# A LoRA linear layer over eight batches: seven block products per pair of batches instead of eight, and router and attention moved into the second phase

## The chip, the cores and the metric

The kernel runs on 1 core of one Trainium2 chip. Its time is the device time of one execution in microseconds (us). Everything below speaks of that one core: TensorE (PE) multiplies, its weight loads run beside it (PEld), VectorE (DVE), ScalarE (ACT) and GpSimd (POOL) work on tiles of 128 partitions, SyncE (SP) issues loads. ScalarE issues the stores.

## What is computed

Eight batches of 512 tokens with 2048 features go through a linear layer with bias and a LoRA term (rank 16, one adapter for each batch). The result h then goes through a small network. All arrays are float32.

```python
h   = x @ W.T + bias + (x @ A[id].T) @ B[id].T            # D_IN = D_OUT = 2048, rank 16
q   = h @ Wq.T                                            # 64 wide
top, idx = top_k((q @ Wr.T) @ (keys @ Wr.T).T / sqrt(48) + log_rel, 8)
w   = softmax(q . keys[idx] / 8 + log_rel[idx])
aux = (w . values[idx]) @ Wvd.T @ Wvu.T                   # 512 slots, 128, 2048
u   = clip(0.5 * log1p(var(h)) / mean(log1p(var(h))) + 2.5 * sigmoid(gelu(h @ Wu1.T + bu1) @ Wu2.T + bu2), 0, 5)
gate = sigmoid(0.5 * clip((u - 0.5) / 1.5, 0, 1) - 1), 0 where below 0.05
out = x + h + gate * aux
```

The mean of log1p(var) runs over all tokens of all batches. So no gate, and no output, is known before all of h is.

## The kernel before

Every float32 operand of a large product is split into two parts, a rounded one (hi, written by ScalarE, `to_hi`, L426) and the rest (lo, written by VectorE, `lo`, L688). Each product is made of three matmuls: hi by hi, hi by lo, lo by hi. Activations are held transposed, 128 features on the partitions by 512 tokens, in 16 k-tiles for each batch (`xh`, `xl`).

**First phase**, `row(b, ...)`, one row for each of 8 batches: for each of 16 output tiles o it runs 16 k-steps of three matmuls (L1109 to L1111), one matmul that adds the LoRA term (L1128), and then ScalarE takes the tile out of PSUM with the bias (L572). A weight tile is loaded, split and used once for each batch. VectorE makes the residual x + h (`residual`, L793, L796), the sums of h and h squared (L844, L854) and the lo part of h. Both h and the residual are stored. In the same row TensorE multiplies h by Wq (`query_pass`, L1045, L1046), and, for the batch before, makes the router scores and the attention scores together (`scores`, L1066 to L1069, once in four output tiles), turns the weights (`transposes`, L1075) and multiplies them by the values (`z_pass`, L1087). VectorE picks the eight largest scores (`selected`, `masked`, L723 to L737).

**Second phase**, `row2(c, ...)`: for each batch h is loaded and split again, and 16 k-steps of 12 matmuls make h @ Wu1.T in four banks (`u1_pass`, L1165 to L1167). For the batch before come the gate (`gate_dve`, `gate_act`, with four turns of the gate, L1186) and the 16 output tiles of three matmuls each (`aux_pass`, L1199 to L1201), to which VectorE adds the stored residual (L948, L940).

The order on each engine is the order in which the code is written, and semaphores hold one engine for another; nothing is scheduled by a tool. The router and attention of one output tile stand on TensorE as one block:

```python
pe.matmul(sc_ps[:], qa[:, tok], g_a[:], start=True, stop=False)
pe.matmul(sc_ps[:], qb[:, tok], g_b[:], start=False, stop=True)
pe.matmul(at_ps[:], qa[:, tok], k_a[:], start=True, stop=False)
pe.matmul(at_ps[:], qb[:, tok], k_b[:], start=False, stop=True).then_inc(scores_done, 1)
```

Of the kernel before, what the change touches and what calls it, by code (L numbers as in the profile page):

```python
# [3 lines left out]

# [10 lines left out]

P = 128
D = 2048
KT = D // P  # L20
NB = 8
S = 512
TT = S // P
RANK = 16
REP = 3
KL = REP * 2 * RANK
BOT = 64
RDIM = 48
SLOTS = 512
VB = 128  # L30
FU = D // 4
FT = FU // P
NTOK = NB * S
WCOL = D + BOT
WHALF = D // 2
NXR = 8
NTILES = NB * KT
SENTINEL = -3.0e38
MASKED = -1.0e30


def bass_adaln_ffn(
# [20 lines left out]
    f32 = mybir.dt.float32  # L63
# [3 lines left out]
    AX = mybir.AxisListType  # L67

    h_dram = nc.dram_tensor("h_dram", (NB, KT, P, S), f32, kind="Internal").ap()
    r_dram = nc.dram_tensor("r_dram", (NB, KT, P, S), f32, kind="Internal").ap()  # L70

    ctx = ExitStack()
    with ctx:
        def sb(name, shape, dt=f32):
            return ctx.enter_context(nc.sbuf_tensor(name, shape, dt))

# [3 lines left out]
        def wait(eng, semaphore, value):  # L80

            if isinstance(value, int) and value <= 0:
                return
            eng.wait_ge(semaphore, value)


        margin = sb("margin", [P, 480])
        xh = sb("xh", [P, KT, S], f32r)
        xl = sb("xl", [P, KT, S], f32r)
        xraw = sb("xraw", [P, NXR, S])  # L90

        a_sp = sb("a_sp", [P, KT, REP, 2, RANK], f32r)
        b_raw = sb("b_raw", [KL, S])
        b_sp = sb("b_sp", [KL, 2, S], f32r)
        ax_sp = sb("ax_sp", [KL, S], f32r)
        stage = sb("stage", [P, 4, S])
        h_sp = sb("h_sp", [P, 2, 2, S], f32r)
        sq = sb("sq", [P, S])
        sum_h = sb("sum_h", [P, S])
        sum_hh = sb("sum_hh", [P, S])  # L100
        qa = sb("qa", [P, S], f32r)
        qb = sb("qb", [P, S], f32r)
        rep = sb("rep", [P, S])
        att = sb("att", [P, S])

        wt_sp = sb("wt_sp", [P, 2, TT, 2, P], f32r)
        g_a = sb("g_a", [P, SLOTS], f32r)
        g_b = sb("g_b", [P, SLOTS], f32r)
        k_a = sb("k_a", [P, SLOTS], f32r)
        k_b = sb("k_b", [P, SLOTS], f32r)  # L110
        v_sp = sb("v_sp", [P, 2, TT, VB], f32r)
        z_all = sb("z_all", [P, NB, S])
        wsp = sb("wsp", [P, 2, 2 * WCOL], f32r)
        wraw = sb("wraw", [P, 2, WHALF + BOT])
        a_raw = sb("a_raw", [P, KT, RANK])
# [24 lines left out]
        gt = sb("gt", [P, TT])  # L140
# [3 lines left out]

        gact = wraw[:].rearrange("p a n -> p (a n)")[:, 0:FT * S].rearrange("p (m s) -> p m s", m=FT)
        acc = sum_h
        zg = sq
        z_sp = wsp[:, 1, 0:2 * S].rearrange("p (a s) -> p a s", a=2)
        wvu_hi = wsp[:, 0, 0:D]
        wvu_lo = wsp[:, 0, WCOL + BOT:WCOL + BOT + D]  # L150

        r_last = [xraw[:, 4 + o, :] for o in range(4)] + [xraw[:, o, :] for o in range(4)] \
            + [z_all[:, b, :] for b in range(NB - 1)] + [rep[:]]
        h_in = xraw[:, 0:4, :]
        r_in = xraw[:, 4:8, :]
# [1137 lines left out]
```

## Time and profile before

| | |
|---|---|
| median of 3 runs | 2120.66 us (2119.83 to 2120.81) |
| the profiled execution: time, span of its records | 2120.01 us, 2118.2 us |
| busy: PE, PEld, DVE, ACT, POOL | 2095.7, 1728.6, 1217.3, 793.2, 2.5 us |
| granted TensorE clock | 0.999 of full |
| first and second phase (first matmul of the second phase) | 0 to 1649.3 us, 1649.3 to 2118.2 us |
| DMA | 359.47 MB, mean 170 GB/s |

The span is counted from the first to the last instruction on the core; 1.8 us of the execution lie around it. A matmul's duration in the records (some 390 ns) is longer than its share of the engine, since the next one begins before it ends. What one costs in a row of them is the distance of their starts.

### The profile page before, as it was taken

To read this page: it belongs to the slowest core of one execution; us is meant where nothing else is said; L and a number is where in the kernel's file an instruction comes from. 1 tells how busy PE (TensorE), PEld (TensorE's weight loads), DVE (VectorE), ACT (ScalarE), POOL (GpSimd) and SP (SyncE) were. 2 spreads that over 40 slices of the span, in tenths; PEclk is the share of its full clock that TensorE was granted. 3 is DMA by queue.
4 is the path that set the end of the run, shared out by engine and by line. 5 is a ranking of instruction groups with operands and counts; after the bars stand their busy time and mean duration, and the time that the engine had idled before them with its cause. 6 is when DMAs were issued, how large, how long until landed. Compare 5 with 4: busy or idle time off the path is not lost.

```text
span 2118.2 us, 25447 instructions
## 1 busy us (share of the span) xinstructions
PE 2095.7 (99%) x9510; PEld 1728.6 (82%) x9510; DVE 1217.3 (57%) x1995; ACT 793.2 (37%) x1193; POOL 2.5 (0%) x10
## 2 busy tenths in 40 slices
PE   7999999999999999999999999999999999999998
PEld 5888788888888888888888888888888788888886
DVE  4544655665575556656665565557556744444445
ACT  4433533443353334333533353335334432222221
POOL 0000000000000000000000000000000000000000
PEclk9999999999999999999999999999999999999999
DMA  7444544453445444544553445345444366666668
GB/s 247 170 157 155 174 157 138 139 195 126 145 153 180 137 132 164 168 145 136 162 171 127 154 141 190 129 145 172 157 139 136 125 190 222 221 222 218 220 227 304
DMA packets 161009, 359.47 MB, mean 170 GB/s; under 512 B 21172, under 2 KB 22196, under 8 KB 160758
## 3 DMA queue, kind: packets, MB, share of 16 engines
q1 hardware_dynamic: 105590, 257.16, 38.6%
q10 hardware_dynamic: 55296, 100.69, 12.4%
q8 instruction: 75, 1.23, 0.2%
q14 instruction: 48, 0.39, 0.1%
HBM read 257.11 MB, written 100.66 MB: 169 GB/s over the span
## 4 chain that ended last, share of the span: by engine, by line
PE 95%; DVE 2%; DMA 1%; ACT 1%; issue 0%; SPq 0%; ACTq 0%; DVEq 0%
PE bank L1109 22%; PE bank L1111 21%; PE bank L1110 21%; PE bank L1165 6%; PE bank L1167 5%; PE bank L1166 5%; PE bank L1128 1%; PE bank L1045 1%; PE bank L1046 1%; PE bank L1035 1%; PE bank L1036 1%; PE bank L1201 1%; PE bank L1200 1%; PE bank L1199 1%; PE bank L1087 1%; PE bank L1075 1%
## 5 line engine op out<-in xcount | busy, mean ns | idle before, releaser
L1109 PE MATMUL bank<-xh,wsp 128*128 128x512 f32 x2048 | 803.2, 392 | 2.8 <-DVE wsp L688 1.6
L1111 PE MATMUL bank<-xh,wsp 128*128 128x512 f32 x2048 | 798.1, 390 | 0.0
L1110 PE MATMUL bank<-xl,wsp 128*128 128x512 f32 x2048 | 797.7, 389 | 0.0
L1109 PEld LDWEIGHTS bank<-xh,wsp 128*128 128x128 f32 x2048 | 384.9, 188 | 83.5 <-DVE wsp L688 2.5
L1111 PEld LDWEIGHTS bank<-xh,wsp 128*128 128x128 f32 x2048 | 384.7, 188 | 81.3
L1110 PEld LDWEIGHTS bank<-xl,wsp 128*128 128x128 f32 x2048 | 385.1, 188 | 78.6
L688 DVE TENSOR_TENSOR wsp<-wraw,wsp 128x1024 fp32r<-128x1024 f32 (+1 forms) x387 | 322.5, 887 | 181.8 <-ACT wsp L426 181.8
L426 ACT ACTIVATE wsp<-wraw 128x1024 fp32r<-128x1024 f32 (+1 forms) x258 | 266.9, 1079 | 358.4 <-PE bank L1046 357.1
L793 DVE TENSOR_TENSOR stage<-stage,xl 128x512 f32<-128x512 f32 x128 | 88.6, 692 | 447.6 <-ACT stage L572 447.6
L572 ACT ACTIVATE stage<-bank,bias_sb 128x512 f32<-128x512 f32 x128 | 88.1, 688 | 543.1 <-PE bank L1128 543.1
L1165 PE MATMUL bank<-h_sp,xh 128*128 128x512 f32 x512 | 201.7, 394 | 1.9 <-DVE h_sp L688 1.9
L1167 PE MATMUL bank<-h_sp,xl 128*128 128x512 f32 x512 | 200.2, 391 | 0.0
L1166 PE MATMUL bank<-h_sp,xh 128*128 128x512 f32 x512 | 199.9, 390 | 0.0
L426 ACT ACTIVATE h_sp<-xraw 128x512 fp32r<-128x512 f32 x128 | 80.7, 630 | 275.2 <-DVE stage L948 165.0
L948 DVE TENSOR_TENSOR stage<-bank,xraw 128x512 f32<-128x512 f32 x112 | 76.8, 691 | 97.1 <-PE bank L1201 97.1
L688 DVE TENSOR_TENSOR h_sp<-xraw,h_sp 128x512 fp32r<-128x512 f32 x128 | 88.3, 690 | 74.3 <-ACT h_sp L426 74.3
L1165 PEld LDWEIGHTS bank<-h_sp,xh 128*128 128x128 f32 x512 | 96.6, 189 | 22.4 <-DVE h_sp L688 2.8
L1167 PEld LDWEIGHTS bank<-h_sp,xl 128*128 128x128 f32 x512 | 96.4, 188 | 20.4
L1166 PEld LDWEIGHTS bank<-h_sp,xh 128*128 128x128 f32 x512 | 96.6, 189 | 19.7
L688 DVE TENSOR_TENSOR xl<-xraw,xh 128x512 fp32r<-128x512 f32 x136 | 86.1, 685 | 13.1 <-ACT xh L426 13.1
L796 DVE TENSOR_TENSOR stage<-stage,xh 128x512 f32<-128x512 f32 x128 | 88.6, 692 | 4.4
L426 ACT ACTIVATE xh<-xraw 128x512 fp32r<-128x512 f32 x136 | 81.7, 628 | 24.9 <-DMA xraw<-in_x 21.1
(137 smaller groups left out, 1676.5 us busy)
## 6 DMA issues: line engine op xcount, KB each, us to landing
wraw<-in_w SPq DMA_DIRECT2D x129, 544.0 KB, 4.8
wraw<-in_w SPq DMA_DIRECT2D x129, 512.0 KB, 3.5
xraw<-in_x SPq DMA_DIRECT2D x136, 256.0 KB, 5.1
h_dram<-stage ACTq DMA_DIRECT2D x128, 256.0 KB, 2.0
r_dram<-stage ACTq DMA_DIRECT2D x128, 256.0 KB, 2.3
xraw<-h_dram SPq DMA_DIRECT2D x128, 256.0 KB, 3.1
xraw<-r_dram SPq DMA_DIRECT2D x120, 256.0 KB, 3.9
out<-stage ACTq DMA_DIRECT2D x112, 256.0 KB, 4.0
```

What stands on the lines that cost most here:

```text
L426: return act.activation(dst, src, ACT.Copy)
L572: act.activation(stage[:, slot, :], main_ps[slot][:], ACT.Identity, bias=bias_sb[:, o:o + 1]).then_inc(h_ready, 1)
L688: return dve.tensor_tensor(dst, src, hi.bitcast(f32), SUB)
L793: dve.tensor_tensor(r_tile, h_tile, xl[:, o, :].bitcast(f32), ALU.add)\
L796: dve.tensor_tensor(r_tile, r_tile, xh[:, o, :].bitcast(f32), ALU.add)\
L948: dve.tensor_tensor(stage[:, o % 4, :], aux_ps[o % 2][:], r_in[:, o % 4, :], ALU.add)\
L1109: pe.matmul(acc_ps, w_hi, xh[:, k, :], start=(k == 0), stop=False)
L1110: pe.matmul(acc_ps, w_hi, xl[:, k, :], start=False, stop=False)
L1111: last_k = pe.matmul(acc_ps, w_lo, xh[:, k, :], start=False, stop=False)
L1165: pe.matmul(u_ps[m][:], xh[:, k, f], h_sp[:, slot, 0, :], start=(k == 0), stop=False)
L1166: pe.matmul(u_ps[m][:], xh[:, k, f], h_sp[:, slot, 1, :], start=False, stop=False)
L1167: last = pe.matmul(u_ps[m][:], xl[:, k, f], h_sp[:, slot, 0, :], start=False, stop=(k == KT - 1))
```

## The change

The program is written anew; its parts are these.

**Seven products.** Batches 2p and 2p + 1 form pair p. With x in halves of its features (x11, x12 of the first batch, x21, x22 of the second) and W.T in four blocks B11, B12, B21, B22, the four blocks of h come from seven products of 8 output tiles by 8 k-tiles each, in this order on TensorE (S and T are sums of blocks):

| | x operand | w operand | what follows |
|---|---|---|---|
| M1 | x11 | B11 | kept by ScalarE in u_t |
| M2 | x12 | B21 | h = M1 + M2 (first batch, first half) |
| M6 | S2 = x22 + S3 | T2 = B22 - T1 | U = M1 + M6 |
| M7 | S3 = x21 - x11 | T3 = B11 - T2 | V = U + M7 |
| M4 | x22 | T4 = B21 - T2 | h = V + M4 (second batch, first half) |
| M5 | S1 = x21 + x22 | T1 = B12 - B11 | h = V + M5, and U4 = U + M5 |
| M3 | S4 = x12 - S2 | B22 | h = U4 + M3 (first batch, second half) |

Each output tile has 8 k-steps of three matmuls. The main PSUM banks are four instead of two, the weight tiles in SBUF three instead of two (each 128 x 1024), the x tiles 12 (in place of 16).

**Who makes the sums.** The T blocks are made once, in pair 0, by GpSimd (40 subtractions of 128x1024), and T1 to T4 are stored in DRAM and loaded by the later pairs. The S blocks (32 sums of 128x512 for each pair) are made by GpSimd in the first pair and by VectorE in the other three.

**The first phase** (`for g in range(TILES)`, 224 tiles of 24 matmuls) has otherwise the splits, the LoRA products, the sums of h and its squares, and the store of h. The residual is neither made nor stored.

**The second phase** (`for step in range(ROWS * KT)`) now has, beside the 12 matmuls of a k-step, the Wq product (2 matmuls in each step), and for the batch before the router scores, the attention scores, the turns, the values product and the gate, which is multiplied into the attention weights. The output tiles of a batch come 31 steps after its first k-step, one for each step, into one PSUM bank (four banks at the end). GpSimd adds x and h, both loaded (`r_h`, `r_x`, L763), and VectorE adds the product (`add_out`, L1387).

The core of the new code:

```diff
+M1, M2, M6, M7, M4, M5, M3 = range(NPROD)
...
+                for k in range(HT):
+                    i = x_index(p, q, k)
+                    if k == 0:
+                        pe.wait_ge(wl_ready, g + 1)
+                    if o == 0:
+                        pe.wait_ge(xl_ready, i + 1)
+                    f = slice(k * P, (k + 1) * P)
+                    pe.matmul(ps, wsp[:, slot, 0, f], x_hi(i), start=(k == 0), stop=False)
+                    pe.matmul(ps, wsp[:, slot, 0, f], x_lo(i), start=False, stop=False)
+                    last = pe.matmul(ps, wsp[:, slot, 1, f], x_hi(i), start=False, stop=(k == HT - 1))
...
+            for g in range(TILES):
+                p, q, o = tile_of(g)
+                if p == 0 and q == M1:
+                    if o == 0:
+                        make_t1(0)
+                    if o < HT - 1:
+                        make_t1(o + 1)
+                    make_s3(0, o)
+                if p == 0 and q == M2:
+                    make_t2(o)
...
+                if p > 0 and q == M2:
+                    make_s2(p, o)
+                if p > 0 and q == M4:
+                    make_s1(p, o)
+                if p > 0 and q == M5:
+                    make_s4(p, o)
+                if q == M3 and p < NPAIR - 1:
+                    make_s3(p + 1, o)
...
+        SCORE_AT = {1: 0, 4: 1, 7: 2, 10: 3}
+        TURN_AT = {3: 0, 6: 1, 9: 2, 12: 3}
+        Z_AT = {7: 0, 13: 1}
+        AUX_LAG = 2 * KT - 1
...
+                if c < NB:
+                    h_lo(step)
...
+                    if k in SCORE_AT:
+                        selected(b * TT + SCORE_AT[k])
+                        masked(b * TT + SCORE_AT[k])
+                    if k - 1 in SCORE_AT:
+                        normalise(b * TT + SCORE_AT[k - 1])
+                    if k in TURN_AT:
+                        wt_lo(b * TT + TURN_AT[k])
+                    if k in Z_AT:
+                        z_lo(b, Z_AT[k])
+                a = aux_of(step)
+                if a is not None:
+                    add_out(a)
...
+                if c < NB:
+                    u_pass(step)
+                    query_pass(step)
+                if 1 <= c <= NB and k in SCORE_AT:
+                    attention_pass(b * TT + SCORE_AT[k])
```

In this extract the first `for g` loop is GpSimd's, `if p > 0` stands in VectorE's loop, and the last lines are TensorE's.

**Where instructions move: TensorE, one group of scores.** Before, the two router and the two attention matmuls stand together, in the first phase, between two output tiles, and the next main matmul waits for a weight tile and for its bank (`g_a`, `g_b` are the router's keys, `k_a`, `k_b` the attention's):

```order
L1128 MATMUL bank<-ax_sp,b_sp 128x512 [waits bl_ready]
L1066 MATMUL bank<-g_a,qa 128x512 [waits topk]
L1067 MATMUL bank<-g_b,qb 128x512
L1068 MATMUL bank<-k_a,qa 128x512
L1069 MATMUL bank<-k_b,qb 128x512
L1109 MATMUL bank<-xh,wsp 128x512 [waits wl_ready,h_ready]
L1110 MATMUL bank<-xl,wsp 128x512
```

In the changed kernel they stand in a k-step of the second phase, the router's in front of the 12 matmuls with Wu1 and the two with Wq, the attention's behind them (the lines between are left out):

```order
L1623 MATMUL bank<-z_sp,wvu_sp 128x512 [waits out_ready,zl_ready]
L1624 MATMUL bank<-z_sp,wvu_sp 128x512
L1625 MATMUL bank<-z_sp,wvu_sp 128x512
L1586 MATMUL bank<-g_a,qa 128x512 [waits topk,qh_ready,qab_ready]
L1587 MATMUL bank<-g_b,qb 128x512
...
L1566 MATMUL bank<-h_sp,wq_sp 128x512
L1567 MATMUL bank<-h_sp,wq_sp 128x512
L1593 MATMUL bank<-k_a,qa 128x512 [waits topk]
L1594 MATMUL bank<-k_b,qb 128x512
L1623 MATMUL bank<-z_sp,wvu_sp 128x512 [waits out_ready,zl_ready]
```

Router and attention share one bank (`s_ps`), so the attention waits for VectorE's second step on the router's scores (`topk`), and behind it stands an output tile that waits for VectorE's addition of the one before (`out_ready`).

**VectorE, the same group.** Before, the operations on the scores are followed by the lo part of the next weight tile:

```order
L723 MAX top<-bank 128x8
L713 MEMSET carrier 128x1 [waits topk]
L726 MATCH_REPLACE rep<-top,bank 128x512
L731 TENSOR_SCALAR rep<-rep 128x512 [waits topk]
L735 TENSOR_TENSOR att<-bank,rep 128x512 [waits wt_done,topk]
L737 TENSOR_REDUCE nmax<-att 128x1 [waits topk]
L688 TENSOR_TENSOR wsp<-wraw,wsp 128x1024 [waits wh_ready]
```

Now they stand in front of the addition of an output tile and the lo part of h of the next step (`h_sp`), and the first operation on the attention's scores waits for `at_done`, the end of the attention matmuls:

```order
L1295 MAX top_61<-bank 128x8
L1276 MEMSET carrier 128x1 [waits topk]
L1298 MATCH_REPLACE rep<-top_61,bank 128x512
L1300 TENSOR_SCALAR rep<-rep 128x512 [waits topk]
L1306 TENSOR_TENSOR att<-bank,rep 128x512 [waits wt_done,at_done,topk]
L1308 TENSOR_REDUCE nmax<-att 128x1 [waits topk]
L1387 TENSOR_TENSOR o_st<-bank,r_h 128x512 [waits out_in1,r_ready,aux_done]
L1061 TENSOR_TENSOR h_sp<-hraw,h_sp 128x512 [waits hh_ready]
```

**SyncE at the start.** Before, a weight tile's load waits only for VectorE's lo part of an earlier one:

```order
L336 DMA z_all<-in_values_t 128x512
L296 DMA wraw<-in_w 128x1024 [waits wl_ready]
L296 DMA wraw<-in_w 128x1088 [waits wl_ready]
L336 DMA z_all<-in_values_t 128x512
L296 DMA wraw<-in_w 128x1024 [waits wl_ready]
```

Now each weight load of the first product also waits for GpSimd's T block of the tile before it in that place (`t_ready`), and the other operand of the next T block is loaded behind it (`t_res`):

```order
L507 DMA wraw<-in_w 128x1024 [waits t_ready,wl_ready]
L545 DMA t_res<-in_w 128x1024
L530 DMA xraw<-in_x 128x512 [waits xl_ready] x3
L507 DMA wraw<-in_w 128x1024 [waits t_ready,wl_ready]
L545 DMA t_res<-in_w 128x1024
```

## Rows read from the trace of the kernel before

**Rows 1.** The page: busy time by engine, 40 slices, the chain by engine

```profile
PE 2095.7 (99%) x9510; PEld 1728.6 (82%) x9510; DVE 1217.3 (57%) x1995; ACT 793.2 (37%) x1193; POOL 2.5 (0%) x10
...
GB/s 247 170 157 155 174 157 138 139 195 126 145 153 180 137 132 164 168 145 136 162 171 127 154 141 190 129 145 172 157 139 136 125 190 222 221 222 218 220 227 304
...
PE 95%; DVE 2%; DMA 1%; ACT 1%; issue 0%; SPq 0%; ACTq 0%; DVEq 0%
```

**Rows 2.** TensorE's timeline, end of an output tile and turns: start, busy, operation

```profile
469.66 0.39 PE L1111 MATMUL bank<-xh,wsp 128*128 128x512 f32 x1
...
472.38 0.39 PE L1111 MATMUL bank<-xh,wsp 128*128 128x512 f32 x1
472.61 0.40 PE L1128 MATMUL bank<-ax_sp,b_sp 96*128 96x512 f32 x1
472.84 0.60 PE L1075 MATMUL bank<-ident,att 128*128 128x128 f32 x4
473.20 0.47 PE L1109 MATMUL bank<-xh,wsp 128*128 128x512 f32 x1
```

**Rows 3.** TensorE's timeline elsewhere: values, z and learned matmuls

```profile
85.15 1.05 PE L1024 MATMUL bank<-z_all 128*128 128x128 f32 x8
...
1678.43 1.60 PE L1087 MATMUL bank<-wt_sp,v_sp 128*128 128x256 f32 x12
...
1711.60 0.95 PE L1177 MATMUL bank<-ones,sum_h 128*128 128x1 f32 x8
```

**Rows 4.** TensorE's waits: line waited for, total, times, longest

```profile
PE bank L1035 <- DVE a_sp L688: 8.6, 1, 8.6
```

**Rows 5.** Groups by line and form: busy, mean ns of one, idle before

```profile
L688 DVE TENSOR_TENSOR wsp<-wraw,wsp 128x1024 fp32r<-128x1024 f32 x258 | 314.9, 1221 | 178.8 <-ACT wsp L426 178.8
L426 ACT ACTIVATE wsp<-wraw 128x1024 fp32r<-128x1024 f32 x129 | 136.7, 1059 | 357.7 <-PE bank L1046 357.1 <-DMA wraw<-in_w 0.6
L426 ACT ACTIVATE h_sp<-xraw 128x512 fp32r<-128x512 f32 x128 | 80.7, 630 | 275.2 <-DVE stage L948 165.0 <-PE bank L1167 109.1 <-DMA xraw<-h_dram 1.1
L948 DVE TENSOR_TENSOR stage<-bank,xraw 128x512 f32<-128x512 f32 x112 | 76.8, 691 | 97.1 <-PE bank L1201 97.1
```

**Rows 6.** VectorE's timeline: one group of scores before the change

```profile
297.56 0.69 DVE L723 MAX8 top<-bank 128x8 f32<-128x512 f32 x1
...
298.37 0.68 DVE L726 MATCH_REPLACE8 rep<-top,bank 128x512 f32<-128x512 f32 x1
...
299.55 0.69 DVE L735 TENSOR_TENSOR att<-bank,rep 128x512 f32<-128x512 f32 x1
300.28 0.69 DVE L737 TENSOR_REDUCE nmax<-att 128x1 f32<-128x512 f32 x1
300.88 2.48 DVE L688 TENSOR_TENSOR wsp<-wraw,wsp 128x1024 fp32r<-128x1024 f32 x3
```

**Rows 7.** Timelines of ScalarE and VectorE: gelu of a row and one gate

```profile
1703.22 1.28 ACT L615 ACT_TABLE_LOAD   x1
1704.52 2.53 ACT L615 ACTIVATE wraw<-bank,bu_sb 128x512 f32<-128x512 f32 x4
...
1712.58 0.26 ACT L629 ACTIVATE sg<-bank,bu_half 128x4 f32<-128x4 f32 x1 [2.81 <-PE bank L1177]
...
1714.77 0.16 DVE L923 TENSOR_TENSOR gt<-gt,keep 128x4 f32<-128x4 f32 x1
```

**Rows 8.** GpSimd: groups by form

```profile
L417 POOL MEMSET qb<- 64x512 f32 x1 | 0.5, 525 | 0.1
L419 POOL TENSOR_SCALAR_AFFINE_SELECT ident<-ident 128x128 f32<-128x128 f32 x1 | 0.3, 294 | 0.2 <-POOL k_b L417 0.2
```

**Rows 9.** DMA issues: kind, count, KB each, median us to landing

```profile
wraw<-in_w SPq DMA_DIRECT2D x129, 512.0 KB, 3.5
z_all<-in_wvd_t SPq DMA_DIRECT2D x1, 1024.0 KB, 6.8
```

**Rows 10.** Windows: length, busy (count) by engine, PEclk, DMA share, GB/s

```profile
2100.00:2110.00 10.00, 8.23 (x34) 5.79 (x33) 7.61 (x12) 0.63 (x1) 0.00 (x0) 1.00 0.93 339
```

More of the change, by code:

```diff
@@ new lines, in is_stored, with wait_stored, wait_all_stored @@
+        def is_stored(n):
+            kind, g = entries[n][2:4]
+            return kind == "t4" or kind == "tile" and g < PAIR and tile_of(g)[1] in (M7, M5)
+        def wait_stored(eng, kind, g):
+            n = W_PLACE[kind, g]
+            eng.wait_ge(t_out[n % NWR], 16 * sum(is_stored(i) for i in range(n % NWR, n + 1, NWR)))
+        def wait_all_stored(eng):
+            for place in range(NWR):
+                eng.wait_ge(t_out[place], 16 * sum(is_stored(i) for i in range(place, len(entries), NWR)))
@@ new lines, in _, with load_h @@
+            while nw < len(entries):
+                load_w(nw)
+                nw += 1
+            def load_h(m):
+                c, k = m // KT, m % KT
+                if m < 4:
+                    sp.wait_ge(v_ready, HT * NPAIR)
+                    sp.wait_ge(h_ready, h_index(NPAIR - 1, M5, HT - 1) + 1)
+                wait(sp, hl_ready, m - 3)
+                if k == 0 and c % 2 == 0:
+                    done = 4 * HT * (c // 2 + 1)
+                    for i in range(NST):
+                        sp.wait_ge(h_out[i], 16 * ((done - i + NST - 1) // NST))
+                sp.dma_start(hraw[:, m % 4, :], h_dram[c, k]).then_inc(hr_in[m % 4], 16)
@@ L705, in split_a_lo, with split_w_lo @@
-            def split_a_lo(b):
-                wait(dve, ah_ready, b + 1)
-                for r in range(REP):
-                    last = lo(a_sp[:, :, r, 1, :], a_raw[:], a_sp[:, :, r, 0, :])
-                last.then_inc(al_ready, 1)
+            def split_w_lo(g):
+                p, q, o = tile_of(g)
+                dve.wait_ge(wh_ready, g + 1)
+                src = t_res[:, o, :] if p == 0 and q == M6 else w_raw("tile", g)
+                lo(wsp[:, g % NW, 1, :], src, wsp[:, g % NW, 0, :]).then_inc(wl_ready, 1)
@@ new lines, in stats_pass @@
+            def stats_pass(seg):
+                p, s = seg // 3, seg % 3
+                pe.wait_ge(sum_ready, 4 * HT * p + (HT, 3 * HT, 4 * HT)[s])
+                wait(pe, stats_ready, seg)
+                for i in range(2):
+                    for t in range(TT):
+                        last = pe.matmul(stat_ps[:, i * TT + t:i * TT + t + 1], sums[:, seg % 2, i, t * P:(t + 1) * P],
+                                         ones[:, 0:1], start=True, stop=True)
+                last.then_inc(stats_done, 1)
@@ new lines, in attention_pass, with turn_pass @@
+            def attention_pass(i):
+                t = i % TT
+                pe.wait_ge(topk, TOPK_STEPS * i + 2)
+                tok = slice(t * P, (t + 1) * P)
+                pe.matmul(s_ps[:], qa[:, tok], k_a[:], start=True, stop=False)
+                pe.matmul(s_ps[:], qb[:, tok], k_b[:], start=False, stop=True).then_inc(at_done, 1)
+            def turn_pass(i):
+                b = i // TT
+                pe.wait_ge(wgt_ready, i + 1)
+                wait(pe, wtl_ready, i)
+                wait(pe, zl_ready, i // 2)
+                pe.wait_ge(tanh_ready, 2 * b + 1)
+                for s in range(TT):
+                    last = pe.transpose(wz_ps[:, s * P:(s + 1) * P], att[:, s * P:(s + 1) * P], ident[:])
+                last.then_inc(wt_done, 1)
```

2037 lines of the change are left out of this document (1167 added, 870 removed).

## The prediction

> **What bounds the kernel now.** I began with the page. TensorE is busy in 99% of the span and makes up 95% of the chain that ended last [rows 1]; VectorE, at 57%, and ScalarE, at 37%, have room. TensorE's waits confirm it: the longest is 8.6 us at the start [rows 4]. So the time is a count of matmuls times the distance of their starts. From 469.66 to 472.38 lie twelve of them: 0.227 us for 512 columns; a LoRA matmul takes 0.23, four turns of weights 0.36 [rows 2]. Eight fp32 records of 128 columns are 1.05 us busy, of which some 0.9 are slots; a z product of twelve matmuls takes 1.6, and four one-column sums 0.95, of which 0.85 are slots [rows 3].
>
> **First phase, to 1649.3 us before.** Main matmuls fall from 6144 to 5376: 768 x 0.227 = **-174**. The Wq product leaves (256 x 0.227 = -58), as do the scores of seven batches (112 x 0.227 = -25), 28 groups of turns (-10) and 14 z products (-22). Sums over features rise from 7 groups of eight to 11, each 1.7: +7. LoRA (384 matmuls) and values (the same columns) stay. Together -282: 1367.
>
> Can the helpers follow? An output tile is 24 x 0.227 = 5.4 us. VectorE's dearest regular step, the last tile of M5, has the lo part of a weight (1.2), the sums (1.2), four x splits, one S sum and two additions from PSUM (about 0.6 each when they follow one another): 6.7 us. It falls back by 1 us, and the next tile has fewer splits; weights are split two tiles ahead. ScalarE needs 1.06 for a weight and 0.63 for an x tile [rows 5]. In pairs 1 to 3 I charge 1 us for the joints. The mean load stays near 200 GB/s (115 MB of weights, 75 of x, some 60 of stores and T blocks, in 1370 us), within what the slices at the end show [rows 1].
>
> The first pair is different. In M1 SyncE waits for GpSimd's T block before it loads the next weight and the next T operand, and that block waits for the operand: a loop of issue (0.9), landing and one GpSimd subtraction. GpSimd has no addition in this trace. Below, it is bounded by writing 512 columns, 0.52 us, so 1.05 for 1024; above, by the affine select, which reads and writes 128 columns in 0.29, so 2.35 for 1024 and 1.18 for 512 [rows 8]. I take the upper, since it reads too. Landing is 3.5 us for 512 KB in calm traffic and 6.8 for 1 MB in the starting burst [rows 9]; I take 5. The loop is then 8.3 us, against 5.4 that TensorE wants. SyncE enters it at about 15 us; seven turns and 7 us for landing and splits make the weight of tile 10 ready at 80 us, wanted at 75. The bytes to that point (19 MB) need 57 us at 339 GB/s [rows 10], so they fit narrowly. I charge **+10** for the pair, with ends 0 (loop of 5.5 us) and +40 (landing 6.8, and as much again in M2, where T2 loads run beside the weights). Start: +1. First phase: 1379.
>
> The Trainium skill (GPSIMD Engine Reference, Elementwise — side-by-side cycle accounting) gives 4497 ns for an addition of 2048 columns on GpSimd; scaled, 2.25 for 1024, which would leave the sum where it is.
>
> **Second phase.** A k-step is now 14 matmuls, 3.17 us; 16 of them 50.8.
> - Row 0: 50.8, 2.7 for sums and mean, and a gap in front. After the last matmul VectorE must finish the tile (0.75), ScalarE square it and split the last Wu1 weights (1.9), then split h (0.63), and VectorE its rest (0.69): 4.3. Total 57.8.
> - Rows 1 to 7, work: 50.8 + 3.6 (scores) + 1.4 (turns) + 3.2 (z) + 0.85 (learned) = 59.9, times 7 = 419; 97 output tiles of 0.68 = 66; other joints 2. Total 487.
> - Rows 1 to 7, **waits**. In a score step TensorE issues the router's matmuls, 3.17 us of others, then the attention's. VectorE's two steps on the router's scores take 1.5 [rows 6] and are hidden. But the attention's result, 0.22 after the issue of its last slot, then goes through the masked addition and the maximum: 0.73 to the start of the second, 0.60 to the next operation [rows 6]. Behind them in VectorE's order stands the addition of an output tile (0.69 [rows 5]), which frees the one bank TensorE wants next. That is 0.2 + 0.73 + 0.60 + 0.69 with two hand-overs: **2.3 us** idle. The lo part of the next h comes 0.6 later, hidden by the three output matmuls (0.68); in row 1, which has no outputs, it takes the addition's place. Steps 4 and 10 cost 2.3, step 7 with its z split 2.65. At a row's start, the gelus end 0.85 after the last matmul, then come a weighted sum (0.8), three query operations across two engines (2.1) and the output addition (0.7): TensorE waits 0.85 in step 1. There the gate (0.26 to 0.16 at 1714.77: 2.35 us from 1712.58 [rows 7]) stands in front of the selection, so the attention comes 0.55 late, and again 2.3. A row loses 10.95; seven lose **76**. Two table loads of 1.28 [rows 7] are new in each row, for gelu and for the exponential; both begin while ScalarE waits anyway, so nothing, or +1.3 a row if not.
> - Row 8 has no Wu1 work to cover anything. It is a chain: start to the first masked scores 13, then three times (score 4.9, exponential and normalising 1.7, turn and two splits 3.0, output additions between 5), z 1.6 and splits: 57.
> - Row 9: 15 output tiles, each with 0.75 MB to load and store. At 339 GB/s [rows 10] one takes 2.2, less what is loaded ahead: 30 with the last store.
>
> Second phase 57.8 + 487 + 76 + 57 + 30 = 708, where before it was 469.
>
> **Sum.** 1379 + 708 = 2087 of span, and 1.8 around it: 2089. The profiled execution took 2120.0, 0.65 under the median, so I forecast **2089** beside 2120.66.
>
> **Rivals.** A time within 0.2%, 2116.4 to 2124.9, is what a measurement of this kernel can hardly tell from no change.
> 1. *VectorE's masked steps are hidden after all*, for instance because TensorE has queued work enough. Then the 76 go: 2013. For it: the same steps cost nothing before. Against it: before, the work behind them had other banks and a weight split long in advance; the order now puts one bank and one h split behind them. A partial form lies near 2050.
> 2. *GpSimd's additions hold VectorE off.* Place: the second phase, where each of 128 output tiles has one addition by GpSimd of two tiles in SBUF, beside VectorE's h split, and pair 0 with 72 sums. If each of the 97 in rows 1 to 7 delayed what TensorE waits for by its own 1.18 us: +114, 2203. Only where VectorE is already late (28 score steps and 7 row starts): +41, 2130. It decides from 24 such delays on, (2117 - 2089) / 1.18. Against it: by my step times the addition for tile a + 4 falls after the loads that follow tile a's own addition, away from the critical splits. For it: nothing in the trace, where GpSimd stands still after 3.5 us. The Trainium skill (SBUF — State Buffer, SBUF: two separate sides) says that a VectorE operation with two SBUF inputs and a GpSimd operation that reads SBUF exclude each other for a whole instruction; by that rule this rival holds wherever the two meet. No row here shows it.
> 3. *The first pair starves.* With landings of 6.8 and the loop through M2 the pair costs 40 instead of 10, and S sums come late: 2119, within 2110 to 2135.
> 4. *The change does less than it says*: the order of TensorE lists 5376 main matmuls, so this is excluded.
>
> **How the numbers follow.** The forecast has 0.58, with 2065 to 2115 for the waits (28 x 0.5) and the two last rows (10 each). Rival 1 has 0.10, rival 2 0.20, rival 3 0.12 (0.02 faster, 0.06 same, 0.04 slower). Faster: 0.58 + 0.10 + 0.02 = 0.70. Same: 0.06. Slower: 0.24. For 8 in 10 the range leaves out most of rival 1 and the upper half of rival 2: 2040 to 2150.
>
> **What would show it.** The first phase should end near 1379 us, its second to fourth pairs at about 332 each (56 x 5.44, 27 for LoRA and sums) with TensorE full; the first some 20 longer. In score steps TensorE should wait 2.3 us for the output addition (L1387) or the h split (L1061), 28 times, and rows 2 to 7 be 82 us long. A GpSimd addition should take 1.2 and 2.3. I am wrong if VectorE's h split shows twice its 0.69, if GpSimd's T subtractions run past 3 us, if pairs 1 to 3 show waits, or if rows 2 to 7 last 71 or over 88 us.

## The result, and the profile after

The changed kernel took **2238.5 us** (median of 4 runs, 2234.3 to 2242.2) against 2120.7 for the kernel before: a ratio of **1.0555**, 95% interval 1.0536 to 1.0574. The forecast was 2089 within 2040 to 2150, with 0.24 on slower. It was wrong by 149 us and by its sign.

The profiled execution took 2238.93 us, its span is 2237.1. The page answers to [rows 1]:

```profile
PE 2029.8 (91%) x8682; PEld 1625.9 (73%) x8682; DVE 1253.1 (56%) x1728; ACT 686.5 (31%) x1035; POOL 331.1 (15%) x211
...
PEclk9889989999999999999999999999999898998956
```

828 matmuls fewer, and yet TensorE is busy for only 66 us less. The line of the clock says why: the granted TensorE clock was 0.999 of full on average before and is 0.944 now, with dips in the first six slices and in the last twelve. A busy time in the records says nothing of the clock at which it was spent.

Where the time went is read from windows. The first answer has the four pairs of the first phase (LoRA's first matmul to the next pair's). The second has stretches of the second phase: row 0, row 1, then rows 3 and 6, and last rows 8 and 9 to the last matmul. (Columns as in [rows 10]; a row is counted from its gelus.)

```profile
10.90:422.30 411.40, 353.49 (x1472) 281.39 (x1473) 249.58 (x226) 121.95 (x170) 158.99 (x74) 0.93 0.66 224
422.30:775.20 352.90, 351.01 (x1530) 278.84 (x1529) 207.19 (x253) 127.04 (x183) 0.00 (x0) 1.00 0.57 188
775.20:1108.50 333.30, 333.30 (x1490) 272.38 (x1489) 203.64 (x248) 118.92 (x167) 0.00 (x0) 1.00 0.54 182
1108.50:1445.80 337.30, 332.98 (x1487) 271.84 (x1486) 204.03 (x248) 123.36 (x175) 0.52 (x1) 1.00 0.55 181
```

```profile
1445.80:1499.40 53.60, 53.60 (x233) 44.46 (x234) 15.27 (x28) 12.92 (x20) 0.00 (x0) 0.94 0.27 79
1499.40:1572.20 72.80, 62.89 (x293) 50.38 (x292) 35.68 (x78) 22.69 (x42) 5.30 (x4) 1.00 0.30 90
1662.90:1752.20 89.30, 77.56 (x338) 62.39 (x337) 48.65 (x93) 23.42 (x42) 21.00 (x16) 0.94 0.56 188
1937.00:2029.10 92.10, 80.48 (x338) 64.79 (x337) 47.43 (x93) 23.34 (x42) 21.54 (x17) 0.91 0.54 182
2123.10:2227.70 104.60, 60.60 (x168) 39.37 (x166) 44.61 (x87) 13.70 (x25) 33.24 (x26) 0.62 0.57 194
```

Pairs 2 to 4 run as forecast: 333.3 us of full TensorE in pair 3; in pair 2 some 17 more for the values and a wait of 2; in pair 4 a gap of 4.7 in front of the second phase. The whole excess over the forecast span (2237 - 2087 = 150 us) sits in three places:

| place | forecast | measured | excess |
|---|---|---|---|
| first phase to its last matmul; all of it in the first pair | 1379 | 1441.1 | 62 |
| row 0 with the gap in front | 57.8 | 58.3 | 0.5 |
| rows 1 to 7 | 563 | 623.7 | 61 |
| rows 8 and 9 to the end of the span | 87 | 114 | 27 |

**Rows 1 to 7: the waits are those forecast.** TensorE's waits from the first output matmul of row 2 to the end of row 7 (line, releaser, total, times, longest):

```profile
PE bank L1623 <- DVE o_st L1387: 64.8, 30, 2.6
PE bank L1566 <- DVE rep L1284: 6.2, 6, 1.4
```

One of them in full, in row 6, first VectorE and then TensorE (start, busy, engine, line, operation). The masked addition and the maximum wait for the attention's scores, the addition for out (L1387) stands behind them, and the output matmul (L1623) waits for that:

```profile
1955.00 0.69 DVE L1306 TENSOR_TENSOR att<-bank,rep 128x512 f32<-128x512 f32 x1 [1.72 <-PE bank L1594]
1955.72 0.69 DVE L1308 TENSOR_REDUCE nmax<-att 128x1 f32<-128x512 f32 x1
1956.33 0.68 DVE L1387 TENSOR_TENSOR o_st<-bank,r_h 128x512 f32<-128x512 f32 x1
```

```profile
1957.15 0.76 PE L1623 MATMUL bank<-z_sp,wvu_sp 128*128 128x512 f32 x1 [2.25 <-DVE o_st L1387]
1957.71 0.63 PE L1624 MATMUL bank<-z_sp,wvu_sp 128*128 128x512 f32 x1
1958.14 0.63 PE L1625 MATMUL bank<-z_sp,wvu_sp 128*128 128x512 f32 x1
...
1959.85 0.63 PE L1551 MATMUL bank<-h_sp,wu 128*128 128x512 f32 x1
1960.28 0.48 PE L1552 MATMUL bank<-h_sp,wu 128*128 128x512 f32 x1
1960.59 0.40 PE L1553 MATMUL bank<-h_sp,wu 128*128 128x512 f32 x1
1960.82 0.40 PE L1551 MATMUL bank<-h_sp,wu 128*128 128x512 f32 x1
```

The wait is 2.25 us, the 2.3 of the forecast. What follows was in no term of it: the next matmuls start 0.43 us apart instead of 0.23 (0.56 behind the very first), 512 columns at 1.2 GHz instead of 2.4. So the wait is paid again in part. In a row at a granted clock of 0.91, (1 - 0.91) x 92.1 = 8 us of TensorE's work are lost, and that lifts a row of 82 to 90 of the 92 measured.

Not every pause is followed by half clock. These are the stretches behind three pauses of row 6 (steps 1, 7 and 10) and, last, one in row 1 of a later run, a2, whose second phase is the same code:

```profile
1957.00:1963.00 6.00, 5.85 (x19) 4.75 (x20) 2.51 (x6) 0.89 (x3) 1.28 (x1) 0.72 0.82 253
1992.90:1999.00 6.10, 6.01 (x28) 5.01 (x29) 2.44 (x6) 1.35 (x3) 1.54 (x2) 1.00 0.84 289
2008.00:2014.00 6.00, 5.54 (x18) 4.49 (x19) 2.83 (x6) 1.20 (x3) 1.33 (x2) 0.72 0.71 265
...
1518.00:1524.00 6.00, 5.77 (x20) 4.67 (x21) 1.44 (x4) 0.84 (x3) 0.00 (x0) 0.72 0.34 87
```

The longest pause of row 6, 2.97 us from start to start in step 7, is the one without. Over rows 2 to 7 half clock follows 16 of the 18 pauses of 2.64 us, one of the six of 2.97, and each of the six row starts. At a row's start stand two shorter pauses close together, 1.2 to 1.8 us for the queries and 1.86 for the output product, and there TensorE runs at half clock for up to 6.8 us. So the length of a pause alone does not decide. Rows 8 and 9, where TensorE stands idle for 44 of 104.6 us, run at 0.62.

**The first pair** has a granted clock of 0.93, and TensorE waits long where it hardly does in later pairs. Up to the pair's end the waits are

```profile
PE bank L1513 <- DVE xop L1061: 41.5, 7, 13.7
PE bank L1513 <- DVE wsp L1061: 11.2, 3, 7.7
PE bank L1441 <- DVE u_t L1109: 10.0, 3, 6.7
PE bank L1513 <- ACT u_t L776: 2.8, 1, 2.8
```

In the second line 7.7 us are for the very first weight, before this window; the rest, with 1.5 for LoRA, is 59 us (pair 2 has 1.9, pairs 3 and 4 none). Half clock adds less than 0.93 suggests: of 61 us at half clock some 27 lie in the pauses themselves, where no matmul is slowed, and the other 34 cost 17. The two, 59 and 17, are nearly all that the pair's 411.4 is above pair 3's 333.3.

The longest wait, 13.7 us at 72.3, is at the start of M2: the x12 tiles 4 to 7 stand in SyncE's queue behind the loop of T operands, in which SyncE waited 39.2 us for GpSimd:

```profile
SPq L468 <- POOL t_res L672: 39.2, 7, 6.7
```

Most of the others are at the starts of M6, M7 and M5 and within M5. Around the first of those VectorE and then GpSimd show

```profile
129.41 3.41 DVE L1061 TENSOR_TENSOR wsp<-t_res,wsp 128x1024 fp32r<-128x1024 f32 x1
132.74 0.74 DVE L1129 SCALAR_TENSOR_TENSOR stage<-bank,bias_sb,u_t 128x512 f32<-128x512 f32 x1
134.55 2.86 DVE L1143 TENSOR_TENSOR sums<-sums,stage 128x1024 f32<-128x1024 f32 x1 [1.07 <-ACT stage L855]
137.33 2.28 DVE L1061 TENSOR_TENSOR wsp<-t_res,wsp 128x1024 fp32r<-128x1024 f32 x1
139.53 7.27 DVE L1061 TENSOR_TENSOR xop<-xraw,xop 128x512 fp32r<-128x512 f32 x3
```

```profile
128.33 3.40 POOL L678 TENSOR_TENSOR t_res<-wraw,t_res 128x1024 f32<-128x1024 f32 x1
131.70 2.27 POOL L710 TENSOR_TENSOR xraw<-xraw,v_t 128x512 f32<-128x512 f32 x1
133.93 2.40 POOL L678 TENSOR_TENSOR t_res<-wraw,t_res 128x1024 f32<-128x1024 f32 x1
```

A split of 1024 columns, 1.22 us in [rows 5], takes 3.41; three x splits, 2 us otherwise, take 7.27; the addition from PSUM at 132.74 keeps its 0.74, though GpSimd works beside it. VectorE's operations with both inputs in SBUF and GpSimd's take turns. The Trainium skill (SBUF — State Buffer, SBUF: two separate sides) says just this, an exclusive lock for the whole instruction; by that rule, the trace agrees.

### The profile page after: what moved, and what is told of

It reads as the page before. It is cut to its first block and busy times, and to the rows that moved or that the text cites. A ratio compares the mean times of both kernels' runs of the same rounds, so it can differ in the third digit from the quotient of the medians.

```text
span 2237.1 us, 24897 instructions
## 1 busy us (share of the span) xinstructions
PE 2029.8 (91%) x8682; PEld 1625.9 (73%) x8682; DVE 1253.1 (56%) x1728; ACT 686.5 (31%) x1035; POOL 331.1 (15%) x211
## 5 line engine op out<-in xcount | busy, mean ns | idle before, releaser
L1513 PE MATMUL bank<-xop,wsp 128*128 128x512 f32 x1792 | 715.8, 399 | 55.6 <-DVE xop L1061 41.5
L1514 PE MATMUL bank<-xop,wsp 128*128 128x512 f32 x1792 | 705.6, 394 | 0.0
L1515 PE MATMUL bank<-xop,wsp 128*128 128x512 f32 x1792 | 704.0, 393 | 0.0
L1513 PEld LDWEIGHTS bank<-xop,wsp 128*128 128x128 f32 x1792 | 340.4, 190 | 144.5 <-DVE xop L1061 46.3
L1514 PEld LDWEIGHTS bank<-xop,wsp 128*128 128x128 f32 x1792 | 341.1, 190 | 74.7 <-issue 3.8
L1515 PEld LDWEIGHTS bank<-xop,wsp 128*128 128x128 f32 x1792 | 340.3, 190 | 73.5
L1061 DVE TENSOR_TENSOR wsp<-wraw,wsp 128x1024 fp32r<-128x1024 f32 x216 | 275.7, 1276 | 169.6 <-ACT wsp L769 169.1
L769 ACT ACTIVATE wsp<-wraw 128x1024 fp32r<-128x1024 f32 x216 | 227.9, 1055 | 294.8 <-PE bank L1515 264.1
L763 POOL TENSOR_TENSOR r_h<-r_h,r_x 128x512 f32<-128x512 f32 x128 | 168.8, 1319 | 623.1 <-DMA r_h<-h_dram 623.1
L1551 PE MATMUL bank<-h_sp,wu 128*128 128x512 f32 x512 | 218.4, 427 | 13.6 <-DVE h_sp L1061 13.6
L1552 PE MATMUL bank<-h_sp,wu 128*128 128x512 f32 x512 | 212.3, 415 | 0.0
L1553 PE MATMUL bank<-h_sp,wu 128*128 128x512 f32 x512 | 210.9, 412 | 0.0
L1143 DVE TENSOR_TENSOR sums<-sums,stage 128x1024 f32<-128x1024 f32 x116 | 151.8, 1309 | 92.4 <-ACT stage L855 92.3
L1061 DVE TENSOR_TENSOR xop<-xraw,xop 128x512 fp32r<-128x512 f32 x192 | 147.2, 797 | 35.3 <-ACT xop L769 34.6
L1623 PE MATMUL bank<-z_sp,wvu_sp 128*128 128x512 f32 x128 | 63.2, 494 | 100.9 <-DVE o_st L1387 100.9
L1551 PEld LDWEIGHTS bank<-h_sp,wu 128*128 128x128 f32 x512 | 105.3, 206 | 38.7 <-DVE h_sp L1061 16.2
L769 ACT ACTIVATE xop<-xraw 128x512 fp32r<-128x512 f32 x192 | 114.9, 620 | 52.2 <-DMA xraw<-in_x 21.7
L1552 PEld LDWEIGHTS bank<-h_sp,wu 128*128 128x128 f32 x512 | 105.4, 206 | 22.7
L1553 PEld LDWEIGHTS bank<-h_sp,wu 128*128 128x128 f32 x512 | 103.9, 203 | 24.5
L1387 DVE TENSOR_TENSOR o_st<-bank,r_h 128x512 f32<-128x512 f32 x128 | 87.7, 685 | 60.2 <-PE bank L1625 46.5
```

The source lines that it names most:

```text
L763: pool.tensor_tensor(r_h[:, a % 4, :], r_h[:, a % 4, :], r_x[:, a % 4, :], ADD).then_inc(r_ready, 1)
L769: return act.activation(dst, src, ACT.Copy)
L1061: return dve.tensor_tensor(dst, src, hi.bitcast(f32), SUB)
L1143: dve.tensor_tensor(into, into, stage[:, n % NST, :, :], ADD).then_inc(sum_ready, 1)
L1387: dve.tensor_tensor(o_st[:, a % 4, :], aux_bank_of(a)[:], r_h[:, a % 4, :], ADD).then_inc(out_ready, 1)
L1513: pe.matmul(ps, wsp[:, slot, 0, f], x_hi(i), start=(k == 0), stop=False)
```

## The experiments

Ratios are to the kernel before, with 95% intervals; 2238 us is the changed kernel's time. "Time at half clock" is worked out from a stretch's granted clock, 2 x (1 - clock) x length.

### Rows 1 to 7: what a wait costs

**b1_masked_later**, the wait taken away:

```diff
                     if k in SCORE_AT:
                         selected(b * TT + SCORE_AT[k])
-                        masked(b * TT + SCORE_AT[k])
                     if k - 1 in SCORE_AT:
+                        masked(b * TT + SCORE_AT[k - 1])
                         normalise(b * TT + SCORE_AT[k - 1])
```

> The masking of a score tile (its addition and its maximum, which wait for the attention scores at the end of the step) is moved on VectorE to the next step, behind the split of the next h tile; so the addition for out of the same step no longer stands behind it. Nothing else is changed. Theory A (each wait of 2.3 to 2.65 us in a score step is paid twice, once as the wait and once as the half clock that TensorE was granted behind it): the 28 waits of rows 1 to 7 go (28 x 2.4 = 67 us) and so do the stretches at half clock behind them (some 8.5 us a row, 60 us): rows 2 to 7 last about 73 us instead of 91, and the whole about 2238 - 125 = 2113 us. Theory B (the half clock has another cause, such as the power that the denser rows draw): only the waits go, about 2171 us, with rows of 81 to 82 us that still show some 17 us each at half clock. Theory C (another wait takes the place of this one, since VectorE is then late for the weights' sum): over 2190 us.

Measured: 2154.4 us, 1.0154 (1.0137 to 1.0171), 84 us off. TensorE's waits over rows 2 to 7:

```profile
PE bank L1623 <- DVE o_st L1387: 20.6, 29, 1.5
PE bank L1566 <- DVE rep L1284: 5.6, 6, 1.1
```

Rows 2 to 7 last 80.1 us on average instead of 91.8, with some 6 us each at half clock instead of 16. Neither pure case: about a third of the waits came back one step later (theory C in part), since the addition for out now stands behind the masking in step k + 1. The clock's share (10 us less at half clock, 5 us of time, in each of six rows) is in the 84.

**b2_fill**, the wait kept and TensorE kept working in it:

```diff
                     attention_pass(b * TT + SCORE_AT[k])
+                    if c < NB:
+                        fill(16)
...
+            def fill(count):
+                for _ in range(count):
+                    pe.matmul(q_ps[:, 0:2 * P], k_a[:, 0:P], zero[:].to_broadcast([P, 2 * P]), start=False, stop=False,
+                              skip_group_check=True)
```

> The waits stay; TensorE fills each of them in rows 1 to 7 with 16 matmuls of 256 columns whose moving operand is zero, added into the queries' bank (nothing changes there). Theory A (the half clock comes from TensorE standing still in the waits): the time of the waits stays (rows keep about 73 us of other work and 9 of fill), but the stretches at half clock in rows 1 to 7 go, so the whole falls by 50 to 60 us to about 2182 us. Theory B (the half clock has another cause): no gain, 2235 us or more, and up to 2260 us if the added matmuls end later than the waits.

Measured: 2207.0 us, 1.0397 (1.0380 to 1.0414), **31 us faster for 448 matmuls more**. VectorE's order is left alone, and so is the time at which it frees the bank: from the last attention matmul to the output matmul it is 2.64 us (2.97 in step 7) as before. Row 2:

```profile
1581.00:1667.00 86.00, 80.11 (x400) 66.62 (x400) 47.27 (x93) 23.45 (x42) 20.90 (x16) 1.00 0.59 196
```

The granted clock is 1.00 here and some 0.98 over rows 2 to 7, which last 86.5 us instead of 91.8. That the half clock in the score steps comes from TensorE standing still is shown by this: 24 us at half clock are left in rows 2 to 7 of 96, all behind the row starts, which were not filled. The gain is half of the 50 to 60 forecast: the 96 us can give back 48 at most, the row starts keep 12 of them, and 32 were seen in the row lengths. What a pause must be like to bring the clock down is not shown. Row 1 has four pauses of 2.5 to 2.9 us from one matmul's start to the next, where later rows have 2.6 to 3.0, and a clock of 1.00 throughout; yet in a2, a3 and a4, with the same code in row 1, half clock does follow its pause of 2.88. What tells the cases apart was not tried.

**b3_no_radd**, the rival of GpSimd's additions, where they meet VectorE in the second phase (`r_h = r_h + r_x` replaced by a memset of one column; x is missing from the output):

> GpSimd's additions of x and h in the second phase are left out (x is missing from the output). If they hold VectorE off and so lengthen the waits of rows 1 to 7, the rows fall by some us each and the whole by over 20 us; by the theory that the rows are bound by the order of VectorE's work and by TensorE's clock, it is within 5 us of 2238, apart from the last two rows, where the addition stands in the chain to the output (up to 15 us).

Measured: 2219.8 us, 1.0467 (1.0450 to 1.0485): 19 us off, between the two expectations, and not in the last rows but at 3 us a row in rows 2 to 7. The scores' waits are untouched (64.7 us in 30). What goes is the one at a row's start, `PE bank L1566 <- DVE rep L1284` of 6.2 us in all. There, in the changed kernel, VectorE's weighted sum of the gelus meets two of GpSimd's additions (VectorE, then GpSimd):

```profile
1939.60 3.31 DVE L1359 SCALAR_TENSOR_TENSOR acc<-gact,wu_sb,acc 128x512 f32<-128x512 f32 x3
```

```profile
1937.18 1.44 POOL L763 TENSOR_TENSOR r_h<-r_h,r_x 128x512 f32<-128x512 f32 x1 [2.41 <-DMA r_h<-h_dram]
1939.66 1.83 POOL L763 TENSOR_TENSOR r_h<-r_h,r_x 128x512 f32<-128x512 f32 x1 [1.04 <-DMA r_h<-h_dram]
```

Without them one such step takes 0.75, with them 1.10 on average here. With that us gone the first of the two pauses at the row's start disappears, the time at half clock in rows 2 to 7 falls from 96 us to 61, and the granted clock over two rows is 0.94 instead of 0.91. So most of the 19 us is clock. Rival 2 is real in this phase, at six places and not at every tile.

### The first pair

**a2_t_ahead**, SyncE's loop opened, GpSimd's sums left as they are:

```diff
-            load_t(0)
+            for i in range(3):
+                load_t(i)
...
+                if g + 3 < HT:
+                    load_t(g + 3)
                 while nw < len(entries) and entries[nw][0] <= g + 1:
                     load_w(nw)
                     nw += 1
-                if g < HT - 1:
-                    load_t(g + 1)
```

> The eight loads of w blocks that the first T sums need are issued three ahead on SyncE, so that its loop in M1 of the first pair no longer holds their landing; GpSimd still makes all sums. If the loop is the cause of the first pair's loss: the steps of 8.3 us become the 5.4 us of a product's tile, the wait of 14 us at the start of M2 goes, and the pair is 14 to 35 us shorter: 2204 to 2224 us. If the loss is GpSimd's sums holding VectorE off, M1 and M2 gain under 10 us and the other gaps (at M6, M7 and in M7, 5 to 8.5 us each) stay: about 2230 us.

Measured: 2217.2 us, 1.0454 (1.0436 to 1.0471), 21 us off. The wait of 13.7 us is 3.1, the pair lasts 388 us instead of 411. The loop was over a third of the pair's excess; the other gaps stay.

**a3_all_vec**: besides, the functions `make_t1` to `make_t1_again`, and `make_s1` to `make_s4` for the first pair, are called from VectorE's program instead of GpSimd's. Two more things differ: in the last five products of this pair (not four) SyncE loads the x tiles of a step ahead of its w tiles, and the last T1 blocks are made one tile later.

> As the run before, and all sums of the first pair, S and T, are made by VectorE too; GpSimd makes none in the first phase. (SyncE loads the x tiles of a step ahead of its w tiles in the last four products of this pair, which the order of VectorE's work needs.) If GpSimd's use of SBUF beside VectorE is what cost the rest of the first pair, its sums fall from 3.1 to 1.2 us, VectorE's own splits go back from 2.0 to 1.2 us, the gaps of 5 to 8.5 us at the products' starts go, and the first pair takes some 350 us instead of 414: about 2175 us. If VectorE has no room for 72 sums more (some 75 us in 340), new waits for its splits of w come up and the pair stays over 390 us: 2210 us or more.

Measured: 2207.3 us, 1.0396 (1.0379 to 1.0413), the pair 382 us. Against a2 that is 10 us, and 6 in the pair. The expected times of the operations came: VectorE's groups up to the second pair are

```profile
L1018 DVE TENSOR_TENSOR wsp<-wraw,wsp 128x1024 fp32r<-128x1024 f32 x50 | 61.1, 1222 | 18.9 <-ACT wsp L726 18.8
L1018 DVE TENSOR_TENSOR xop<-xraw,xop 128x512 fp32r<-128x512 f32 x56 | 36.8, 687 | 10.4 <-ACT xop L726 10.2
```

where the changed kernel had

```profile
L1061 DVE TENSOR_TENSOR wsp<-wraw,wsp 128x1024 fp32r<-128x1024 f32 x50 | 72.6, 1452 | 49.5 <-ACT wsp L769 49.2
L1061 DVE TENSOR_TENSOR xop<-xraw,xop 128x512 fp32r<-128x512 f32 x56 | 58.3, 1069 | 34.9 <-ACT xop L769 34.6
```

The sum over the pair is what to look at. VectorE was busy 249.6 us with 226 instructions in the changed kernel, and is busy 255.3 with 298 now, this window's row:

```profile
11.00:392.80 381.80, 350.31 (x1472) 279.60 (x1473) 255.27 (x298) 120.88 (x169) 1.05 (x2) 0.96 0.70 241
```

The 72 sums cost it 40 x 1.22 + 32 x 0.69 = 71 us and give back 65. Handing them to GpSimd had taken next to nothing off VectorE, and added 159 us of GpSimd's work, part of it in chains that TensorE waits for. Still, the pair is at 382, not 350, and the gaps at the products' starts only shrank (in M6 from 6.7 us to 5.3, start to start). The first theory had the operations right and not the size.

**a4_s_vec_t_pool**, the S sums on VectorE and the T sums on GpSimd, T loaded ahead:

> T's w blocks are loaded ahead, the S sums of the first pair are made by VectorE, and only the T sums (and, in the first phase, nothing else) stay on GpSimd. The run with no GpSimd sum gave 2207 us, the one with all of them 2217. If the S sums on GpSimd were what stood in the way (they come at the same steps as VectorE's splits of x), this one is like the first, 2203 to 2209 us; if it is the T sums (1024 columns, 2.35 us alone and 3.1 beside VectorE), it stays at 2214 us or more, with splits of w that take 2.0 us; if VectorE was overloaded by the T sums in the run before, it is faster than both, under 2200 us.

Measured: 2220.4 us, 1.0471 (1.0453 to 1.0488), the pair 397 us. SyncE's order is that of a3, so what separates the two by 13 us is the engine of the T sums of 1024 columns (and the tile at which the last are made); their mean on GpSimd stays at 2.4 to 2.9 us. To move the S sums alone gains nothing over a2. VectorE then has more operations that can meet GpSimd's: `xraw<-xraw,v_t`, 0.69 us in a3, takes 1.93 on average.

What keeps the pair at 382 is open. Its remaining waits (33 us) are in M2 and at the starts of M6, M7 and M5 again, and in M2's last tile VectorE does a T and an S sum ahead of the four x splits (1.22 + 0.68 us). Whether that order or the transfers are the cause was not tried apart.

### A version that beats both

**c2_both_orders** joins the first pair of a3 and the masking of b1, and lets the addition for out go first in the step of the masking:

```diff
                     if k - 1 in SCORE_AT:
+                        a = aux_of(step)
+                        if a is not None:
+                            add_out(a)
+                        masked(b * TT + SCORE_AT[k - 1])
                         normalise(b * TT + SCORE_AT[k - 1])
```

> The first pair as in the run with all its sums on VectorE (2207 us), and the masking moved to the next step (which alone took 84 us off); in that next step VectorE adds out before it masks and normalises. If the two parts are independent: 2238 - 31 - 84 = 2123 us; the remaining waits of TensorE for the addition for out in rows 2 to 7 (20.6 us in 29 waits in the run with the masking moved) go too, with the last of the half clock there (3.4 to 6.8 us a row): 2095 to 2105 us, which is under the kernel before. If the waits only move to the turn of the weights, 2115 us or more.

Measured: 2120.1 us, 0.9998 (0.9988 to 1.0007), level with the kernel before. The parts add up (2123 by the sum), but the further gain did not come. The waits for out fell (over the same stretch from 18.9 us in b1 to 7.7), and rows 2 to 7 still last 79.7 us on average, against 80.1: the clock took it back in this execution, with 48 us at half clock in these rows where b1 has 34. In c4, c5 and c6, whose rows 2 to 7 are the same code, it is 31 to 38 us, and a row lasts 78.6 to 78.8.

**c4_tail_filled**, `fill(6)` after each step but the first of row 8:

> As the run beside it, and in row 8 (scores and outputs of the last row, no first-layer products) TensorE makes 6 more matmuls of 256 columns with a zero moving operand at the end of each step. If the clock is what makes rows 8 and 9 take 105 us where 87 were predicted (72 us of them at half clock), the two fall by 8 to 18 us against the run beside it; if they are bound by VectorE's chain and by the transfers for out, no gain, or a loss of up to 10 us by the added matmuls.

Measured: 2119.5 us, 0.9993 (0.9983 to 1.0002); rows 8 and 9 take 101.4 us instead of 101.6, though the time at half clock there fell from 79 us (granted clock 0.61) to 59 (0.71). So these 20 us of half clock cost nothing: of the kernel's own 166 matmuls in this stretch 84 start at half clock instead of 120, which is up to 8 us of TensorE, and the stretch is no shorter. What the other 59 us cost was not tried. In c2 TensorE waits in rows 8 and 9 for

```profile
PE bank L1627 <- DVE o_st L1387: 26.6, 23, 5.7
PE bank L1597 <- DVE rep L1298: 7.9, 4, 3.1
PE bank L1607 <- DVE att L1316: 5.6, 4, 1.9
```

The output matmul waits for VectorE to free the one bank, and VectorE for the matmul.

**c5_more_banks** gives the output tiles four banks from step 2 of row 8 on:

```diff
-            return aux_bank if a < (NB - 1) * KT + 1 else bank[a % 4]
+            return aux_bank if a < (NB - 2) * KT + 3 else bank[a % 4]
...
-                wait(pe, out_ready, a if a <= (NB - 1) * KT else max((NB - 1) * KT + 1, a - 3))
+                wait(pe, out_ready, a if a < (NB - 2) * KT + 3 else max((NB - 2) * KT + 3, a - 3))
```

> As the run with both orders (2120 us); from the third step of row 8 on the products for out go to the four banks of the first layer in turn, which are free by then (before: from row 9 on). So TensorE no longer waits for VectorE's addition of the tile before (26.6 us in 23 waits in rows 8 and 9 of that run). If that ping-pong between the two engines is what makes row 8 long: rows 8 and 9 fall from 102 us towards 80 to 88, and the whole to 2098 to 2108 us, under the kernel before. If the transfers for out bound them (768 KB a tile at the 302 GB/s of the end, 2.6 us each, 81 us for 32 tiles): no less than 2100 us. If VectorE's chain of the scores bounds them, 2115 us or more.

**c6_banks_filled** is the same with `fill(3)` in row 8:

> As the run beside it, with 3 zero matmuls of 256 columns at the end of each step of row 8 but the first. Filling six took under 1 us off before, though it cut the half clock in rows 8 and 9 from 68 to 48 us: the clock did not bind there. With the waits for banks gone it may: 0 to 6 us less than the run beside it; more if TensorE is now what row 8 waits for; 1 to 3 us more if the added matmuls only stand in the way.

The 68 and 48 us at half clock in it should be 79 and 59; the difference is the same.

Measured: c5 **2105.9 us, 0.9934** (0.9920 to 0.9947), with rows 8 and 9 at 89.1 us instead of 101.6; c6 **2103.8 us, 0.9924** (0.9911 to 0.9938). Both beat the kernel before, and the changed one by 6%. The intervals of the two overlap, so what the fill adds here is not settled. TensorE in rows 8 and 9 of c5:

```profile
PE bank L1627 <- DVE o_st L1387: 13.9, 10, 5.7
PE bank L1607 <- DVE att L1316: 10.9, 4, 3.6
PE bank L1597 <- DVE rep L1298: 7.8, 4, 3.1
```

The wait for the addition is halved, the one for the normalised weights (L1607) is up from 5.6 us to 10.9. What is left looks like VectorE's chain of the last row's scores, which was not tested. And the page of c6:

```profile
PE 1995.8 (95%) x8727; PEld 1604.9 (76%) x8727; DVE 1260.7 (60%) x1800; ACT 682.9 (32%) x1035; POOL 172.4 (8%) x140
...
PEclk9989999999999999999999999999999999999987
```

## Why the prediction was wrong

Two steps failed above all: "a row loses 10.95", which priced a wait at its length alone, and the +10 for the first pair. A third, the 57 for row 8, was too short.

- **First phase, matmuls removed: right.** Pair 3, with nothing but products, LoRA and sums in it, lasted 333, where 332 stood.
- **The first pair, +10 with ends 0 and +40: mis-sized, by 62 us.** The loop's step was foreseen closely, 8.3 us where (78.4 - 27.7) / 6 = 8.45 was measured between SyncE's loads behind the sums, but with luck: the landing is 4.6 us instead of 5 and the subtraction 3.2 instead of 2.35. That GpSimd's T subtractions run past 3 us was one of my signs of being wrong, and came true. I asked only when the weight of tile 10 would be ready, and not what else stood in SyncE's queue behind the loop: the x tiles 4 to 7 of M2, whose wait is 13.7 us. To open the loop gave 24 us of the pair. The rest is in the waits at the products' starts, with VectorE and GpSimd taking turns in part of them, and in half clock, 17 us. I had priced GpSimd's operation and left VectorE's own at their lengths of before.
- **"TensorE idle 2.3", 28 times, 76 in all: right as a wait, wrong as a price.** 64.8 us in 30 waits for L1387, 9.3 in row 1 for the h split and 6.8 for the queries were measured, 81 in all. The failed step is "a row loses 10.95": it took an idle us to cost a us. Rows 2 to 7 lost another 5 to 10 each to the clock, about 48 us in all, of which b2 took 31 back with the waits in place. With the 5 us of longer waits that is 53 of the 61; the other 8 were not taken apart. The trace of before could not show this cost, as its clock is 0.999, and I put no bound on it; the sum assumed 0.227 a matmul everywhere.
- **Row 8, 57, and row 9, 30: 27 too short.** The chain's pieces were listed, and add up to over 58, not 57, but the bank shared by sixteen output tiles was charged at "additions between 5"; c5 shows that ping-pong to be worth 12.5 us. The rest is open. Of the half clock there, which looks worst (0.62), 20 us cost nothing that can be measured (c4).
- **Rival 1, the masked steps are hidden:** fell at once. **Rival 3, starving, 2119:** its mechanism took part, the pair costing 72 where the rival had 40. **Rival 2, GpSimd holds VectorE off:** true wherever the two were seen to meet, at 19 us in the second phase (b3) and about 10 in the first pair beyond the loop (a2 to a3). Of its two sizes the lower, +41, was the nearer. Its +114 needed a delay at each tile, and there were six places.
- **"I am wrong if rows 2 to 7 last over 88 us":** they lasted 91.8. The sign of the whole came from two costs of 62 and 61 us that add up, with the tail, to 150.
- **The Trainium skill** has the case that I missed (TensorE: Matmul & The Clock Gate, A second HAM failure mode: psum-queue depth-cycling): a TensorE that micro-idles between groups of matmuls while banks are cycled oscillates between the two clocks. By that rule, rows 1 to 7 cost more than their waits; rows 2 to 7 agree, and row 1, at 1.00 in this run, does not show it.

## What to carry to other kernels

When an edit turns a TensorE that never waits into one that waits often, price each wait twice: by its length, and by the matmuls behind it that may run at half clock (here half clock followed most of the waits, and cost 48 us beside some 80 of waiting); then look in the profile at the granted clock and not at busy time. Before work is given to GpSimd to relieve VectorE, add up VectorE's own time with and without: here 72 sums moved away lengthened the rest by 65 of the 71 us saved. In a chain that can't be shortened, first look for what stands behind it in an engine's order for no reason: one moved line of VectorE's program gave back 84 us.

## What was not expected of the hardware

- TensorE falls to half clock behind waits of 2.25 us, in rows 2 to 7 behind 16 of 18 of them, and also behind two pauses of under 2 us close together at each row's start, but behind only one of six pauses of 2.97 and, in this run, none in row 1. Matmuls of zeros in the waits keep the clock at 1.00 there, and made the kernel 31 us faster.
- A GpSimd subtraction of 1024 columns takes 2.35 to 2.40 us at its shortest and up to 3.4 beside VectorE; one of 512 takes 1.28 and up to 2.27. VectorE's split of 1024 goes from 1.22 to 3.41 around 130 us, its additions from PSUM stay at 0.74.
- Half clock where TensorE waits much (0.62 in rows 8 and 9) was free in part: 20 us less of it changed the time by under 1 us. In the first pair nearly half of it fell into pauses, where no matmul is slowed.
